# Attention edges: the product of a pair waits for its selection, the collection for the product alone

## The reference

```python
h = (x @ W).reshape(n, HEADS, HID)
a_s = jnp.einsum('nhc,hc->nh', h, att_src)
a_d = jnp.einsum('nhc,hc->nh', h, att_dst)
e = jax.nn.leaky_relu(a_s[src] + a_d[dst], NEG_SLOPE)
m = jax.ops.segment_max(e, dst, num_segments=n)
ex = jnp.exp(e - m[dst])
denom = jax.ops.segment_sum(ex, dst, num_segments=n)
alpha = ex / denom[dst]
msg = h[src] * alpha[:, :, None]
out = jax.ops.segment_sum(msg, dst, num_segments=n)
```

## Time and profile before

| | us |
|---|---|
| timed runs, median of 3 | 4394.04 |
| lowest and highest | 4389.03, 4397.5 |
| profiled execution, its span | 4836.3 |
| of it, first attention edge phase (first to last gather) | 1337 |
| of it, second attention edge phase (first to last gather) | 1336 |

### The profile page before, as it was taken

One profiled execution on the slowest core, in us unless ns is written; L12 is line 12 of the kernel. 1 busy time (PEld: TensorE's weight loads), 2 busy tenths in 40 slices (PEclk: granted clock), 3 DMA queues, 4 the chain that ended last, 5 costly groups with the idle time before them and its releaser, 6 DMA issues. The chain is left out here.

```text
span 4836.3 us, 56702 instructions
## 1 busy us (share of the span) xinstructions
PE 3107.3 (64%) x11125; PEld 1876.3 (39%) x11125; DVE 3044.1 (63%) x8069; ACT 2574.7 (53%) x7729; POOL 2895.1 (60%) x2918
## 2 busy tenths in 40 slices
PE   4699999989998883455555555555354555555451
PEld 3344444444444372333333334433233333333331
DVE  7788888878887753455555455566354555555557
ACT  3598888888888642333334334344243334343347
POOL 2366666656665405677777767733676777777763
PEclk8899999999999996677777767778576777767776
DMA  5233323333322244444444444424444444444445
GB/s 165 93 88 87 86 86 86 87 85 86 87 85 84 72 127 134 112 129 118 129 123 124 129 118 129 131 61 127 117 126 121 122 125 128 118 129 124 124 108 161
DMA packets 274567, 540.54 MB, mean 112 GB/s; under 512 B 73156, under 2 KB 161983, under 8 KB 274240
## 3 DMA queue, kind: packets, MB, share of 16 engines
q0 software_dynamic: 134912, 376.36, 28.8%
q1 hardware_dynamic: 132308, 154.29, 10.3%
q10 hardware_dynamic: 7020, 6.40, 0.4%
HBM read 495.47 MB, written 41.31 MB: 111 GB/s over the span
## 5 line engine op out<-in xcount | busy, mean ns | idle before, releaser
L1247 POOL DMA_INDIRECT arena<-h_rows,idx x1856 | 1893.8, 1020 | 972.0 <-issue 515.2
L1382 PE MATMUL ps<-arena,z 128*128 128x264 f32 x3712 | 1328.7, 511 | 493.1 <-DVE arena L1494 290.8
L769 POOL DMA_INDIRECT arena<-y_rows,idx x928 | 901.0, 971 | 717.7 <-ACT arena L800 359.1
L1306 ACT ACTIVATE z<-z 128x256 f32<-128x256 f32 x928 | 382.2, 412 | 1504.0 <-remote 833.3
L1382 PEld LDWEIGHTS ps<-arena,z 128*128 128x128 f32 x3712 | 856.6, 249 | 728.2 <-DVE arena L1494 351.7
L1502 DVE TENSOR_TENSOR z<-ps,z 128x264 f32 x928 | 396.1, 427 | 1105.3 <-remote 713.3
L798 ACT ACTIVATE arena<-arena 128x128 f32<-128x128 f32 x2784 | 912.0, 393 | 110.8 <-DVE arena L885 64.4
L840 PE MATMUL ps<-arena 128*128 128x512 f32 x1856 | 902.5, 610 | 4.6 <-DVE z L893 4.6
L1298 ACT ACTIVATE z<-iota,dst_x 128x128 f32<-128x128 f32 x1856 | 644.5, 395 | 26.4
L1494 DVE TENSOR_TENSOR arena<-arena,z 128x520 f32<-128x520 f32 x928 | 639.0, 689 | 1.8 <-ACT z L1287 1.1
L832 PE MATMUL ps<-arena 128*128 128x512 f32 x928 | 495.6, 617 | 121.2 <-DVE arena L885 85.2
(11 more groups left out here) (231 smaller groups left out, 2838.3 us busy)
## 6 DMA issues: line engine op xcount, KB each, us to landing
z<-lo_rows SPq DMA_DIRECT2D x116, 512.0 KB
arena<-h_rows,idx POOLq DMA_INDIRECT x1856
arena<-y_rows,idx POOLq DMA_INDIRECT x928
z<-seg_rows SPq DMA_DIRECT2D x232, 64.0 KB
h_rows<-arena SPq DMA_DIRECT2D x98, 132.0 KB, 1.8
arena<-h_rows SPq DMA_DIRECT2D x98, 132.0 KB, 3.0
arena<-res_rows SPq DMA_DIRECT2D x98, 128.0 KB, 3.0
z<-in_ea_rows SPq DMA_DIRECT2D x464, 8.0 KB
```

The source lines that it names most:

```text
L769: pool.indirect_dma_start(out=ring[:, r, :], out_offset=None, in_=s.y_rows, in_offset=bass.IndirectOffsetOnAxis(ap=rows_of[:, u, n:n + 1], ...
L1247: pool.indirect_dma_start(out=ring[:, u * SCORED + n, :], out_offset=None, in_=h_rows, in_offset=bass.IndirectOffsetOnAxis(ap=s.idx[:, u, ...
L1306: nc.scalar.activation(sel[:, q % SELS, :, :].rearrange("p k n -> p (k n)"), away[:, q % 2, :, :].rearrange("p k n -> p (k n)"), ACT.Relu, ...
L1382: last = t.matmul(ps[:, bank[q % 4], 0:ROW], sel[:, q % SELS, k, :], ring[:, u * SCORED + 2 * q + k, :], start=(k == 0), stop=(k == 1))
```

## The change

Two waits leave `collect` on PE, and one wait enters `message` on DVE. The selection of a pair is now waited for by its product, and the collection waits for the product alone. That the bank is empty no longer has a wait of its own: on DVE the addition of pair q-4 stands in front of the product of pair q, and the product is waited for.

```diff
             def collect(g, u, q):
                 pair = g * STEPS_IN + q
                 pe.wait_ge(msg_ok, pair + 1)
-                pe.wait_ge(sel_ok, pair + 1)
-                if not (isinstance(g, int) and g == 0 and q < 4):
-                    pe.wait_ge(z_ok, g * ADDS + 1 + q - 3 if q >= 4 else (g - 1) * ADDS + 1 + q - 3 + STEPS_IN)
                 for k in range(2):
...
             def message(g, u, q):
                 if q == 0:
                     dve.wait_ge(ex_ok, g + 1)
                     dve.wait_ge(tail_ok, g + 1)
+                dve.wait_ge(sel_ok, g * STEPS_IN + q + 1)
```

## The result

The changed kernel takes 4424.9 us (median of four runs, 4424.2 to 4427.2) against 4392.0 us for the kernel before (4389.0 to 4397.5): ratio 1.0076, 95% interval 1.0062 to 1.0090. That is 33 us, outside the forecast (4385 to 4403) and 5 us above the range's upper end of 4420.

The account below looks back on a forecast made before the run. The prediction took POOL's gathers to bound the edge phases. Its terms, 0 + 0 + 3 + 0 = +3 us, about 2 showing, gave 4394 + 2 = 4396 us; forecast 4385 to 4403 (chance 0.62), range 4376 to 4420.

Parts of the forecast that it names:

- The gather is the bound: POOL, edge phases: gathers and the distances between them set the pace but for 110 us a phase of waits for collections.
- The late signals are to a good part a cost of the profile: PE's late signals in the edge phases: largely from profiling, as timed runs were 442 us faster than the profiled execution.
- PE's separate wait: PE, before each collection: removing the wait on selection and bank gives 0 us, at most 18, since the product comes last.
- DVE's wait in the bursts: DVE, successive additions: products waiting for their selections cost 0 us while POOL is behind, 36 us as outer bound.
- What is queued behind the waiting product: DVE, behind product 11 while ACT's source step waits: scans 1.6 us later, covered except at phase ends, +3 us.
- a group needs 24 us of 42, so it is covered: Mid-phase: the 1.6 us delay costs nothing, as POOL needs the delayed collections only two groups later.
- The load of the block numbers: PE's sequencer: the 1.93 us load can start while the product is awaited, hiding at most 186 us; taken as 0.
- The slower one: Rival, chance 0.23: compute sets the timed runs' pace and the serial hop is paid, 4418 to 4436 us.
- The faster one: Rival, chance 0.15: PE's load and separate wait leave the path of look-ups and collections, about 4368 us.
- What would show it: Signs: POOL still 1.25 us from gather to gather; DVE idle before the product 10 to 30 us a phase, released by selection.

Follow-up runs that it names:

- the second profile: The kernel before, unchanged, profiled again: span 4391.5 us, timed at 4392.7 us, ratio 1.000.
- both_waits: The kernel before plus DVE's wait of the product for the selection, PE keeping its own waits: 4425.5 us, ratio 1.0073.
- source_later: The changed kernel with ACT's source step one place later, behind selection 11: 4392.6 us, ratio 1.0002 against the kernel before.
- the exceptional execution: The first profiled execution of the unchanged kernel before, whose trace the prediction read: span 4836.3 us.
- the earlier trace: The trace of the unchanged kernel before that the prediction read, from its first profiled execution: span 4836.3 us.
- load_first: The changed kernel with DVE's load of eight block numbers for addition 8 issued in front of product 11: 4389.3 us, ratio 0.9995 against the kernel before.
- before_small: The kernel before with each product over 4 of the 65 columns of a head, the rest left out: 4336.3 us, ratio 0.9874.
- before_psum: The kernel before with ACT writing the exponentials into PSUM, collections on two banks instead of four, and no z_ok wait on PE: 4312.0 us, ratio 0.9817.

## Why the prediction was wrong

- **"The gather is the bound."** Right, and more so than it said. The timed runs are at the gather's pace: POOL's idle time for collections is 39 us in both kernels over both phases, in pieces of at most 0.3 us, the ordinary distance of two gathers; so it doesn't wait for them at all.
- **"The late signals are to a good part a cost of the profile."** Wrong as a cause: the second profile spans what the timed runs take. The conclusion drawn from it (the timed runs have no such stops) was right, which was luck as far as the reason goes.
- **PE's separate wait, 0 us.** Right: both_waits, which keeps it, takes as long as the changed kernel, and source_later, which lacks it, as long as the kernel before.
- **DVE's wait in the bursts, 0 of 36 us.** Right in the number: source_later keeps that wait and costs nothing. The rows on which the 36 us were counted came from the exceptional execution; in source_later the selections are ahead, with 0.0 us of idle time before the product.
- **What is queued behind the waiting product.** This is the step that failed. The place was right, L1279 holding back selection 11 in front of product 11. Three things in it were not. First, it stopped 58 groups of 58, not 8. Second, the shift is 0.68 us, not 1.6: the sum added product and addition to the scans' old start of about 1.0 us, but in before too the scans stood behind addition 8, which waits for its collection until 2.81 us, long after the transposition. Third, and what decides, the term ended with "a group needs 24 us of 42, so it is covered". That holds for what POOL waits for; POOL indeed waits no longer. But it took a gather's duration as fixed. The mean of 1022 ns against the 0.94 to 0.95 us of an undisturbed one stood in the earlier trace rows, and the prediction said only that some take longer. At 29 groups a phase, the 55 ns between 1.000 and 0.945 are 51 us, all of them on the path, and which gathers are hit depends on the place of DVE's work. The term was put at +3 us and measured +33, of which 31 are gathers' durations.
- **The load of the block numbers.** The prediction weighed it on PE, where the change takes a wait from in front of it, and not on DVE, where the change puts one in front of it.
- **The rivals.** The slower one had the sign, and its price of 4418 to 4436 covers the result, but for the wrong reason: it was to decide where POOL waits for collections in most groups, and POOL doesn't. The faster one (PE's sequencer) has nothing for it: with PE's waits away and the loss undone (source_later, load_first) the time is that of the kernel before to 0.1%, and with them kept or not beside DVE's wait (both_waits, the changed kernel) it is 4425 us.
- **"What would show it."** 1.25 us from gather to gather was the sign to look at: over a phase it is (941.3 + 928 x 0.30) / 928 = 1.31 us in the changed kernel, 1.30 before. The idle time before the product is 843 us and not 10 to 30 a phase, since the whole stop moved there.

## What to carry to other kernels

When an instruction gets a new wait, list what the sequencer has queued behind it, loads of register values included: they run in the stop's shadow before, and after the stop afterwards. Where one engine's issue rate is the bound, its instructions' mean against the undisturbed duration is a term of its own; ask what runs beside the long ones, and don't call work "covered" that can only lengthen them. A change of order that costs or gains a per cent by where it happens to fall is a hint to remove the collision itself: the exponentials in PSUM are worth 79 us here, more than twice the loss, and make the order matter little (7.7 us instead of 33).

## What the runs showed of the hardware

- An indirect gather of 128 rows takes 0.945 us of POOL and 0.30 us to the next. If a DVE `tensor_tensor` with both inputs in SBUF has begun at least 0.05 us before it and has 0.14 us or more to go, the gather ends 0.81 to 0.83 us after that instruction, up to 1.49 us in all; with a one-hot behind it, up to 1.62. One that begins with the gather or up to 0.12 us after it doesn't hold it (427 of 429). The product isn't lengthened (686 ns before, 687 in the changed kernel). With one input in PSUM nothing is lengthened: 388 gathers, 0.2 us.
- The one-hot, a `tensor_scalar` in bf16 over 2048 columns (0.75 us), has a part in it as well: the gathers beside it have 49 us of lengthening in before_small, where the products are short, and 8 us in before_psum.
- Loading eight block numbers into registers holds DVE's sequencer for 1.83 us (median of 174) and PE's for 1.93 us (median of 116). No busy time shows it, and the idle time behind it is put down to the engine that signalled last.
